# Tempered cross-attention: the sum of the exponentials split between GpSimd and VectorE

## The reference

```python
qk = jnp.einsum('bhqd,bhkd->bhqk', Q, K)
scores = qk / math.sqrt(dk)
mean_sim = scores.mean(axis=(-2, -1))
max_sim = scores.max(axis=-1).mean(axis=-1)
probs = jax.nn.softmax(scores, axis=-1)
entropy_proxy = jnp.var(probs, axis=-1, ddof=1).mean(axis=-1)
feats = jnp.stack([mean_sim, max_sim, entropy_proxy], axis=-1)
hidden = jax.nn.gelu(_linear(feats, w1, b1), approximate=False)
hidden = jax.nn.gelu(_linear(hidden, w2, b2), approximate=False)
log_t = jnp.clip(_linear(hidden, w3, b3), LOG_T_MIN, LOG_T_MAX)
t = jnp.exp(log_t)[..., None]
attn_scores = qk / (2.0 * t)
attn = jax.nn.softmax(attn_scores, axis=-1)
out = jnp.einsum('bhqk,bhkd->bhqd', attn, V)
```

## Time and profile before

| | before |
|---|---|
| median of 3 runs | 3461.16 us (3457.52 to 3462.78) |
| profiled execution | 3467.89 us, span of the engines 3466.1 us |
| busy: PE, PEld | 2943.3 us (85%), 2452.4 us (71%) |
| busy: VectorE | 2398.7 us (69%) |
| busy: ScalarE | 1930.0 us (56%) |
| busy: GpSimd | 1213.2 us (35%) |
| tempered cross-attention | from 2299 us of the span (its memset) to about 2880 us |

### The profile page before, as it was taken

The page is one execution under the profiler, slowest core; times in us unless marked ns, Lnnn a source line. Parts: engine busy times, 40 slices in busy tenths (PEclk is TensorE's granted clock), DMA queues, the critical chain, the costliest instruction groups (busy, mean ns, idle before and its releaser), DMA issues. The chain is left out here.

```text
span 3466.1 us, 75470 instructions
## 1 busy us (share of the span) xinstructions
PE 2943.3 (85%) x24978; PEld 2452.4 (71%) x24978; DVE 2398.7 (69%) x5561; ACT 1930.0 (56%) x4192; POOL 1213.2 (35%) x1172
## 2 busy tenths in 40 slices
PE   5999998799999989579987999956777788899877
PEld 3666666688888878478975777744666567788766
DVE  5777776577777677445657999978788854434387
ACT  3555555466656656345545666656787784224332
POOL 0000000345545555523445565536566660000010
PEclk9999999799999999789998999966898886899998
DMA  4222222000000000123321000000000000000001
GB/s 129 66 64 67 67 67 70 1 2 11 14 11 13 12 11 13 41 96 85 88 79 32 0 0 0 0 1 1 1 2 1 1 2 1 1 0 1 0 21 29
DMA packets 136991, 95.35 MB, mean 28 GB/s; under 512 B 13998, under 2 KB 128787, under 8 KB 136084
## 3 DMA queue, kind: packets, MB, share of 16 engines
q1 hardware_dynamic: 128276, 74.56, 7.3%
q0 software_dynamic: 8448, 17.32, 1.8%
HBM read 34.88 MB, written 56.95 MB: 26 GB/s over the span
## 5 line engine op out<-in xcount | busy, mean ns | idle before, releaser
L1416 POOL TENSOR_TENSOR a_qk<-a_qkv 128x2048 f32<-128x2048 f32 x64 | 235.5, 3679 | 167.0 <-ACT a_qkv L1391 166.9
L862 POOL TENSOR_TENSOR x_p<-x_p,x_rz 128x1232 f32<-128x1232 f32 x64 | 143.7, 2246 | 325.7 <-DVE x_rz L993 303.2
L1351 PE MATMUL a_ps_s<-a_qk,w_ident 128*128 128x256 f32 x1024 | 233.4, 382 | 2.2 <-POOL a_qk L1416 2.0
L1398 ACT ACTIVATE a_r<-a_o,w_a_rows 128x128 f32<-128x128 f32 x512 | 221.3, 524 | 2.1 <-DVE a_o L1442 2.1
L1351 PEld LDWEIGHTS a_ps_s<-a_qk,w_ident 128*128 128x128 f32 x1024 | 191.0, 192 | 28.1 <-POOL a_qk L1416 4.4
L2231 POOL TENSOR_TENSOR f1c_xr<-f_hi,f_lo 128x512 f32<-128x512 f32 (+1 forms) x16 | 20.5, 1282 | 531.8 <-POOLq L101 423.1
L843 POOL MEMSET x_one<- 128x1 f32 x1 | 0.1, 98 | 588.7 <-POOLq L101 588.7
L459 DVE TENSOR_REDUCE a_nmax<-a_ps_s 128x4 f32<-128x512 f32 x256 | 159.0, 684 | 58.6 <-PE a_ps_s L269 58.6
L1216 POOL DMA_INDIRECT f_yg<-f_rows_out,f_index x128 | 121.7, 951 | 214.8 <-DMA f_rows_out<-f_yo 174.4
L1369 PEld LDWEIGHTS a_ps_y<-w_a_o,a_r 128*128 128x128 f32 x1024 | 123.2, 197 | 83.1 <-issue 68.7
L1369 PE MATMUL a_ps_y<-w_a_o,a_r 128*128 128x128 f32 x1024 | 134.1, 286 | 46.7 <-DVE x L1457 46.5
(11 more groups left out here) (486 smaller groups left out, 9439.6 us busy)
## 6 DMA issues: line engine op xcount, KB each, us to landing
f_rows_out<-a_zeros SPq DMA_DIRECT2D x31, 1088.0 KB, 5.3
f_xin<-f_rows_in SPq DMA_DIRECT2D x135, 64.0 KB
f_rows_out<-f_yo SPq DMA_DIRECT2D x135, 64.0 KB
out<-x SPq DMA_DIRECT2D x16, 256.0 KB, 2.3
f_raw<-in_late_f SPq DMA_DIRECT2D x2, 1408.0 KB, 8.0
w_ctx<-in_ctx SPq DMA_DIRECT2D x1, 2464.0 KB
f_rows_in<-x_xr,x_where POOLq DMA_INDIRECT x128, 2.3
f_yg<-f_rows_out,f_index POOLq DMA_INDIRECT x128, 2.6
```

The costliest lines, as they stand in the source:

```text
L862: nc.gpsimd.tensor_tensor(wide, wide, rz[:, :].unsqueeze(2).broadcast_to([P, HEADS, K]), ALU.mult).then_inc(p_ready, 1)
L1351: ins = nc.tensor.matmul(ps_s[u % 2][:, 0:HEADS * HEADS], c.ident[:, :], qk[:, u % 2, k, :, :], start=k == 0, stop=k == HD - 1)
L1398: ins = nc.scalar.activation(r[:, u % 2, :, :, a], o[:, u % 2, :, :].rearrange("p h d -> p d h"), ACT.Copy, scale=c.w["a1_rows"][:, a:a + 1])
L1416: nc.gpsimd.tensor_tensor(qk[:, u % 2, :, :, :], qkv[:, u, 0, :, :].unsqueeze(3).broadcast_to(full), qkv[:, u, 1, :, :].unsqueeze(2).broad ...
```

## The change

The tile e is widened from 77 to 78 columns a head (HALF = 39, twice), and GpSimd clears it once at the start of the stage, so that the 78th column stays zero; ScalarE's first instruction waits for that clearing too (`cleared`). In each slot GpSimd, between k_bd and sq, adds columns 39 to 77 of each head of e to columns 0 to 38 and writes the result to a new tile `halved` (two buffers, 624 columns), signalling `halved_ready`. VectorE sums `halved` instead of e, waiting for `halved_ready` instead of `e_ready`, and does so after the sum of the squares instead of ahead of it. ScalarE's exponential, which overwrites the tile e of two sequences before, waits for `halved_ready` of that sequence instead of `z_done`.

```diff
--- before.py
+++ after.py
@@ -1474,13 +1474,15 @@
     N = GRP * HEADS
     H = c.w["x1_w2"].shape[0]
     W = 4 * K
+    HALF = (K + 1) // 2
     c.stage = "x1"
     ctx, sb, ps, sem = stage_scope(c)
     with ctx:
         xn, xT, qT, kT = sb("xn", [P, 2, D]), sb("xT", [P, 2, P]), sb("qT", [P, 2, P]), sb("kT", [P, 2, K])
         k_bd = sb("k_bd", [P, 2, GROUP, K])
         d = sb("d", [P, RING, GROUPS, GROUP, K])
-        e, sq = sb("e", [P, 2, HEADS, K]), sb("sq", [P, 2, HEADS, K])
+        e, sq = sb("e", [P, 2, HEADS, 2 * HALF]), sb("sq", [P, 2, HEADS, K])
+        halved = sb("halved", [P, 2, HEADS, HALF])
         v1 = sb("v1", [K, 2, HEADS, STRIP])
         pT = sb("pT", [K, HEADS, P])
         oz, rz, o, oT = sb("oz", [P, 512]), sb("rz", [P, HEADS]), sb("o", [P, 2, D]), sb("oT", [P, P])
@@ -1502,12 +1504,12 @@
...
-                 "oT_ready", "y_ps", "x_done")
+                 "oT_ready", "y_ps", "x_done", "halved_ready", "cleared")
-         oT_ready, y_ps, x_done) = (sem(n) for n in names)
+         oT_ready, y_ps, x_done, halved_ready, cleared) = (sem(n) for n in names)
...
@@ -1615,13 +1617,14 @@
         @block.scalar
         def _(act):
             act.wait_ge(made, 1)
+            act.wait_ge(cleared, 1)
             for t in range(SLOTS):
                 k = gated(t)
                 if (s := step(t, WEIGH)) is not None:
                     act.wait_ge(d_ready, s + 1)
                     wait(act, sq_ready, s - 1)
-                    wait(act, z_done, s - 1)
-                    nc.scalar.activation(e[:, s % 2, :, :], d[:, s % RING, :, :, :].rearrange("p g j k -> p (g j) k"), ACT.Exp,
+                    wait(act, halved_ready, s - 1)
+                    nc.scalar.activation(e[:, s % 2, :, 0:K], d[:, s % RING, :, :, :].rearrange("p g j k -> p (g j) k"), ACT.Exp,
                                          scale=SCALE).then_inc(e_ready, 1)
                 if k is not None:
                     act.wait_ge(f_ps, k + 1)
@@ -1683,6 +1686,7 @@
         @block.gpsimd
         def _(pool):
             nc.gpsimd.memset(v1[:, :, :, :], 1.0).then_inc(made, 1)
+            nc.gpsimd.memset(e[:, :, :, :], 0.0).then_inc(cleared, 1)
             pool.wait_ge(bias_ready, 1)
             for t in range(SLOTS):
                 if (s := step(t, PROJECT)) is not None:
@@ -1693,8 +1697,11 @@
                                             ALU.mult).then_inc(k_bd_ready, 1)
                 if (s := step(t, WEIGH)) is not None:
                     pool.wait_ge(e_ready, s + 1)
+                    wait(pool, z_done, s - 1)
+                    nc.gpsimd.tensor_tensor(halved[:, s % 2, :, :], e[:, s % 2, :, 0:HALF], e[:, s % 2, :, HALF:2 * HALF],
+                                            ALU.add).then_inc(halved_ready, 1)
                     wait(pool, sq_done, s - 1)
-                    nc.gpsimd.tensor_tensor(sq[:, s % 2, :, :], e[:, s % 2, :, :], e[:, s % 2, :, :], ALU.mult).then_inc(sq_ready, 1)
+                    nc.gpsimd.tensor_tensor(sq[:, s % 2, :, :], e[:, s % 2, :, 0:K], e[:, s % 2, :, 0:K], ALU.mult).then_inc(sq_ready, 1)
                 if (s := step(t, TEMPER)) is not None:
                     a, b = row(s)
                     pool.wait_ge(g_ready, s // GRP + 1)
@@ -1731,14 +1738,14 @@
                     dve.wait_ge(max_done, s + 1)
                     nc.vector.tensor_tensor(d[:, s % RING, :, :, :], scores, top.unsqueeze(3).broadcast_to([P, GROUPS, GROUP, K]),
                                             ALU.subtract).then_inc(d_ready, 1)
-                if (s := step(t, WEIGH)) is not None:
-                    a, b = row(s)
-                    dve.wait_ge(e_ready, s + 1)
-                    nc.vector.tensor_reduce(t_z[:, a, b, :], e[:, s % 2, :, :], AX.X, ALU.add).then_inc(z_done, 1)
                 if (s := step(t, SQUARE)) is not None:
                     a, b = row(s)
                     dve.wait_ge(sq_ready, s + 1)
                     nc.vector.tensor_reduce(t_sq[:, a, b, :], sq[:, s % 2, :, :], AX.X, ALU.add).then_inc(sq_done, 1)
+                if (s := step(t, WEIGH)) is not None:
+                    a, b = row(s)
+                    dve.wait_ge(halved_ready, s + 1)
+                    nc.vector.tensor_reduce(t_z[:, a, b, :], halved[:, s % 2, :, :], AX.X, ALU.add).then_inc(z_done, 1)
                 if (s := step(t, PROJECT)) is not None:
                     a, b = row(s)
                     dve.wait_ge(k_ready, s + 1)
```

## The result

The changed kernel takes 3529.9 us (median; 3529.2 to 3531.7), the kernel before, run beside it, 3461.7 (3457.5 to 3462.8). The ratio is 1.0191, with a 95% interval of 1.0177 to 1.0205: 68 us slower, where 56 were forecast. The profiled execution took 3531.7 us with a span of 3529.9, against 3467.9 and 3466.1 before: in spans the difference is 63.8 us.

What follows compares the result with a forecast made beforehand. A closed loop of GpSimd and ScalarE, 7.17 us a slot, was taken as the bound. 52.6 + 1.2 + 2.9 + 2.1 - 4.4 + 2.4 - 0.7 = +56.1 us gave a median of 3517.3; range 3503 to 3546.

Steps and rivals of the forecast that it cites:

- The loop: Ordinary tempered slots: GpSimd's three instructions plus ScalarE's four make 7.17 us; the halving adds 1.46 a slot, +52.6 over 36.
- The rival in which the idle time absorbs the addition: GpSimd's idle 1.66 us takes in the halving, slots stay at 7.17, total 3458; chance 0.04.
- the one in which VectorE is the bound: Rival: each of 64 slots gives back 0.63 us through VectorE's shorter sum, total 3423; chance 0.04.
- The halving's price: GpSimd's 624-column addition: 1.50 us, 1.46 a slot; bounds 1.19 and 2.20.
- The clearing: Start of the stage: ScalarE's first instruction waits for GpSimd's memset of e, about 2.2 us long; +2.1.
- the first slots: Before tempering, VectorE bounds: its round loses 0.63 and becomes 5.02 us; seven intervals, -4.4.
- Slot 14: Slot of the first tempering product; its interval was counted among the seven that lose 0.63 us.
- The gates: Six later gates: VectorE's two-SBUF-operand products meet GpSimd's, x_sims 0.4 us later each, +2.4; first gate, without tempering, -0.7.
- The bound of +1.46: Upper bound for each gate, if x_z waits for both GpSimd products.
- The clock: Rival: PE, less busy, falls to 1.2 GHz and stays; slots 9.5 us, +33 on top, total 3550; chance 0.12.
- three long intervals: Slots of 7.51, 8.55 and 8.86 us with PE at its lower clock become 8.63, 8.63 and 8.86: +1.1, +0.1, 0.
- the tail: After slot 65, two more halvings precede tempering products on which ScalarE waits: 2 x 1.46 = +2.9.

Runs made afterwards that it cites:

- E1: Changed kernel, but VectorE sums the whole 77-column tile e again at its old place and GpSimd's halved tile goes unread; 3529.6 us, ratio 1.0193.
- e3: Kernel before, with GpSimd's tempering product issued ahead of the squares, no halving; 3445.8 us, ratio 0.9950.
- e5: Changed kernel with the halved tile unread, GpSimd's instruction in turn sum of halves, product of halves, lower half plus itself; 3520.1 us (one run).
- e2: Kernel before, but VectorE's sum of squares covers only 39 of 77 columns a head and GpSimd gets no work; 3457.1 us, ratio 0.9992.
- e4: Changed kernel with the tempering product ahead of halving and squares, and VectorE's sum of the halved tile one slot later; 3466.4 us, ratio 1.0015.
- e7: Kernel before, with the gate's reciprocal and product of key means kept in PSUM, so no VectorE instruction there has two SBUF inputs; 3447.2 us, ratio 0.9958.

## Why the prediction was right, and by how much it was off

**The loop: right.** 7.17 us was read as GpSimd's three instructions plus ScalarE's four up to kT. The slots came out at 8.65 where 8.63 was worked out, GpSimd's 1.66 of idle time stayed, ScalarE's wait went to 2.45. 36 slots at 1.475 are 53.1 us, of the 57.3 that the stage became longer; 52.6 were forecast. E1, e3 and e5 show it from three sides: the dead halving costs the same, the other order takes the loop away, and 0.29 us less in the instruction is 0.29 less in the slot. The rival in which the idle time absorbs the addition is out, and so is the one in which VectorE is the bound (e2: 0.63 us less there, the slot the same).

**The halving's price: right.** 1.50 forecast, 1.512 measured. It was taken from sums of two different tensors rather than products with one full operand; e5 shows that the number of different operands is what divides the two lines (1.51 against 1.23, where the product line had given 1.23), and not adding or multiplying. The Trainium skill's figure (GPSIMD Engine Reference, Elementwise — side-by-side cycle accounting: 4497 ns for a float32 add 2048 wide) had given an estimate of 1.37; the trace is 0.14 above it. By that estimate the sum would have been 38 x 0.13 = 5 us less, where the prediction has "some 4".

**The clearing and the first slots: right.** ScalarE's first instruction moved from 2300.05 to 2302.41, by 2.36, for a memset of 2.17; 0.18 of it is that the stage itself began later (GpSimd's first memset at 2299.25 instead of 2299.07). VectorE's shorter sum took 0.80 us (0.79 forecast), the first slots 5.02 (5.02). One step was missed: the intervals into slots 5 and 6 went from 4.53 to 4.74, where GpSimd's own round of 4.73, worked out in the prediction for the later ones, is the bound at once.

**Slot 14: wrong.** It was counted with the first slots at -0.63 and became 6.72 from 5.66. VectorE's x_lt, a tensor_scalar from SBUF to SBUF, took 0.27 us before; the changed kernel's timeline has

```profile
2369.14 2.24 POOL L1704 TENSOR_TENSOR x_sq<-x_e 128x1232 f32<-128x1232 f32 x1
...
2370.46 1.01 DVE L1757 TENSOR_SCALAR x_lt<-x_lt 128x128 f32<-128x128 f32 x1
...
2371.50 0.31 ACT L1684 ACTIVATE x_g<-x_lt 128x128 f32<-128x128 f32 x1 [2.46 <-DVE x_lt L1757]
```

The halving had pushed the squares onto it: x_lt ends right behind them, 4.45 us after the block instead of 3.39, and the interval grew by the same 1.06. In e1, where VectorE does not wait for the halved tile, it is 6.72 too. Against the sum's -0.63 that is 1.7 us.

**The gates: the mechanism right, the size half.** Forecast +0.4 for each, measured +0.47 for four and +1.46 for two, 4.8 us instead of 2.4. Where the forecast held, x_z got in at the end of the squares and x_ent ran into the tempering product:

```profile
2427.76 2.25 POOL L1704 TENSOR_TENSOR x_sq<-x_e 128x1232 f32<-128x1232 f32 x1
...
2429.72 0.44 DVE L1782 TENSOR_TENSOR x_z<-x_t_z 128x128 f32<-128x128 f32 x1
2429.96 2.31 POOL L1710 TENSOR_TENSOR x_d<-x_d,x_g 128x1232 f32<-128x1232 f32 x1
...
2431.18 1.23 DVE L1784 TENSOR_TENSOR x_ent<-x_rec,x_t_sq 128x128 f32<-128x128 f32 x1
```

In the other two x_z was issued 0.5 and 0.3 us later, because PE was late with what the reciprocal reads, and missed that moment. Here is the first:

```profile
2583.80 0.26 DVE L1762 RECIPROCAL x_rz<-x_ps_z 128x16 f32<-128x16 f32 x1 [0.46 <-PE x_ps_z L1611]
...
2584.51 2.25 POOL L1710 TENSOR_TENSOR x_d<-x_d,x_g 128x1232 f32<-128x1232 f32 x1
...
2584.82 2.09 DVE L1782 TENSOR_TENSOR x_z<-x_t_z 128x128 f32<-128x128 f32 x1
```

A difference of 0.3 us in when it was issued decides over 1 us. The bound of +1.46 had this size, with a mechanism that did not occur.

**The clock: wrong, and without a price in the slots.** The prediction named 1.00 between gates as a mark, and a fall there as one of three signs of being wrong. It fell, but not at the price that the rival gave it. Before, all ordinary slots had 1.00 but the first (0.50) and the three long ones; in the changed kernel they go up and down. Windows of two neighbouring slots (the lowest is the second) and of one gate that took 15.19:

```profile
2692.75:2701.41 8.66, 5.53 (x70) 4.50 (x69) 6.57 (x10) 6.20 (x16) 7.00 (x5) 0.91 0.01 2
2701.41:2710.05 8.64, 7.83 (x70) 6.50 (x68) 4.87 (x9) 6.64 (x16) 6.99 (x5) 0.70 0.00 0
...
2580.19:2595.38 15.19, 10.54 (x69) 7.61 (x71) 8.90 (x14) 8.21 (x18) 7.03 (x5) 0.62 0.00 0
```

PE, busy 5.42 us of 7.17 before at 1.00, is busy 5.53 of 8.66 and is granted 0.91, then 7.83 at 0.70, and the slots last the same. The rival's first half came true (the clock falls when PE idles more), its second did not: it fell in parts only, and what PE lost fitted in GpSimd's longer round. It had a price at the gates, where PE's lateness put x_z behind the tempering product: in the first 2 us behind the block PE was granted 0.53 and 0.50 in the two slots that took 15.19, and 1.00 in the four of 14.20. Two of the three long intervals of before became 8.64 as forecast, and the third too (8.86 forecast). The six intervals behind gates changed by -0.4 to +0.8, 1.4 us in all, for which the sum had nothing; in five of them x_lt was held up again, to between 0.42 and 1.10 us.

**The rest.** The stage became 57.3 us longer; with the start (+2.4, 0.2 of it outside of the stage) and the part behind slot 65 (+4.1) that is the 63.8 of the spans. Of the 4.1, 1.9 lie up to the stage's last second exponential (2.9 forecast as the tail); the other 2.3 lie behind the stage, where nothing was changed. The last 4.4 us between 63.8 and 68.2 are no work at all: the profiled execution of before was 6 us above its median, that of the changed kernel 2. The terms of the sum thus miss by some 6 us in the stage (slot 14 by 1.7, slots 5 and 6 by 0.4, the gates by 2.4, the intervals behind them by 1.4), and the median by 12.6.

## What to carry to other kernels

Idle time of an engine that ends with another engine's result is no room for more work: follow that result back, and if it hangs on the same engine's last instruction, everything put in front of that instruction costs its full length, every round (1.51 us of halving, 1.48 us a slot). The order within such an engine is then worth more than the split of work between engines: the tempering product ahead of the squares, with no work saved, made the kernel 0.5% faster (ratio 0.9950), three fifths of it in the ordinary slots, while half a sum less on the busiest engine gave nothing that could be told from no change. When a loop is taken away, look for the next one at once, through the buffers too; here the waits point to a PSUM bank at 6.84 us.

## What the runs showed of the hardware

Two-operand work of VectorE in SBUF beside a busy GpSimd: x_z took 0.29 to 3.95 us by where it fell; with one operand in PSUM it took 0.28 beside the same product. Over all kernels about a hundred such instructions, x_lt (below) among them, were lengthened. Each ended at most 0.16 us behind the end of a GpSimd instruction, nearly always of the one in which it began, even where the next followed without a gap (x_z 0.44 us between squares and tempering product); only at the six gates of e4 did it miss two such ends. The Trainium skill (SBUF — State Buffer, Who interferes with whom) has the lock, and names tensor_scalar too among the instructions that can take the shared ports; the trace agrees in both. The prediction had passed over the second: x_lt, a tensor_scalar from SBUF to SBUF with one tensor operand, went from 0.27 to 1.01 and 2.25 us beside GpSimd's squares and tempering product, and ended with them each time. GpSimd itself lost next to nothing in these meetings (2.31 us instead of 2.25).

GpSimd's elementwise instructions at 624 columns: 1.51 us with two different tensors, 1.23 with one tensor twice, for a sum and a product alike; rows of 39 elements cost nothing extra against the line from whole rows.

PE's granted clock moved in ordinary slots from 1.00 to between 0.70 and 1.00 as its busy share at full clock went from 76% to 64%, without an effect on the slot. Around the gate into slot 45, the shorter gate was followed by PE at half clock where the longer one was not: 1.84 us won, 3.42 lost in the two next intervals. With these gates shortened, the gain measured in the stage alone (16.3 us in e7) was gone beside the other order (484.9 against 482.2).
